# Feed-forward weights loaded in three pieces under cross attention, new orders for its last two steps, and other banks for the first feed-forward tile

## The reference

```
x = layernorm(x + self_attention(x))
x = layernorm(x + cross_attention(x, context) + bo)   # softmax(q k^T / 8) v, then Wo
g = silu(bitlinear(x, w_gate)); u = bitlinear(x, w_up)
x = layernorm(x + bitlinear(g * u, w_down))           # F = 2048
# bitlinear: the rows of x rounded to 8 bits by their own maximum, the weights to -1, 0, 1
```

## Time and profile before

| | us |
|---|---|
| median of 3 runs | 1890.73 (1886.93 to 1893.66) |
| the profiled execution, its own time | 1889.15 |
| its span, first to last instruction | 1887.4 |
| PE busy in the span | 1784.9 (95%) |
| DVE busy | 1445.7 (77%) |
| ACT busy | 1181.5 (63%) |
| POOL busy | 1039.0 (55%) |

### The profile page before, as it was taken

One profiled execution on the slowest core, in us unless ns is written; L12 is line 12 of the kernel. 1 busy time (PEld: TensorE's weight loads), 2 busy tenths in 40 slices (PEclk: granted clock), 3 DMA queues, 4 the chain that ended last, 5 costly groups with the idle time before them and its releaser, 6 DMA issues.

```text
span 1887.4 us, 43032 instructions
## 1 busy us (share of the span) xinstructions
PE 1784.9 (95%) x14128; PEld 1495.1 (79%) x14154; DVE 1445.7 (77%) x3366; ACT 1181.5 (63%) x2696; POOL 1039.0 (55%) x1169
## 2 busy tenths in 40 slices
PE   6899998999999899999999999999999999979997
PEld 4677776777777689999999998899999999964443
DVE  5667667788888777877777788878777877778887
ACT  4676776657656566666666666666566656655664
POOL 0343342334433348767866854587787877542554
PEclk9899998999999899999999999999999999989999
DMA  3322233101103233234324433223313331271221
GB/s 119 119 85 72 65 114 107 39 31 39 49 29 110 86 122 128 75 121 144 98 69 144 130 121 91 79 73 91 110 55 108 91 110 48 66 162 44 64 67 61
DMA packets 109574, 166.80 MB, mean 88 GB/s; under 512 B 32488, under 2 KB 67672, under 8 KB 109512
## 3 DMA queue, kind: packets, MB, share of 16 engines
q1 hardware_dynamic: 91016, 129.77, 22.1%
q0 software_dynamic: 14656, 28.92, 5.5%
q10 hardware_dynamic: 3840, 7.34, 1.2%
HBM read 109.25 MB, written 50.46 MB: 85 GB/s over the span
## 4 chain that ended last, share of the span: by engine, by line
PE 58%; DVE 15%; issue 9%; DMA 7%; ACT 5%; POOL 4%; SPq 1%; POOLq 0%; DVEq 0%; ACTq 0%
PE att_ps_P L1539 5%; PE att_ps_SA L1563 5%; PE att_ps_P L1527 4%; PE att_ps_P L1588 4%; PE att_ps_T L451 3%; PE att_ps_T L1527 3%; PE att_ps_O L1527 3%; PE att_ps_T L1539 3%; PE att_ps_P L1577 3%; DVE sa_sums L751 3%; PE att_ps_O L1539 2%; PE att_ps_P L1599 2%; PE att_ps_SB L513 2%; PE att_ps_T L1588 2%; DMA out_dram<-ff_y_out 2%
## 5 line engine op out<-in xcount | busy, mean ns | idle before, releaser
L1365 POOL TENSOR_TENSOR ca_pr<-ca_pr,ca_rec 112x750 f32<-112x750 f32 x256 | 367.0, 1454 | 212.7 <-DVE ca_rec L1814 209.6
L392 POOL TENSOR_TENSOR sa_p_lo<-sa_pr,sa_p_hi 112x448 fp32r<-112x448 f32 x128 | 147.8, 1160 | 331.7 <-ACT sa_p_hi L599 331.7
L1704 ACT ACTIVATE ca_big<-att_ps_P 126x384 fp32r<-126x384 f32 (+1 forms) x256 | 105.7, 448 | 68.3 <-PE att_ps_P L1577 66.8
L751 DVE RECIPROCAL sa_sums<-sa_sums 128x224 f32<-128x224 f32 x64 | 99.2, 1550 | 47.0 <-ACT sa_sums L608 46.6
L1698 ACT ACTIVATE ca_pr<-att_ps_SA,ca_nmax 112x750 f32<-112x750 f32 x128 | 113.6, 888 | 20.0 <-DVE ca_nmax L1810 9.3
L1819 DVE TENSOR_TENSOR ca_big<-att_ps_P,ca_big 126x384 fp32r<-126x384 f32 (+1 forms) x256 | 120.4, 498 | 4.3 <-ACT ca_big L1704 4.1
L1810 DVE TENSOR_REDUCE ca_nmax<-att_ps_SA 112x1 f32<-112x752 f32 x128 | 119.1, 931 | 0.5 <-PE att_ps_SA L1563 0.4
L1810 DVE TENSOR_REDUCE ca_nmax<-att_ps_SB 112x1 f32<-112x752 f32 x128 | 119.1, 931 | 0.0
L1539 PE MATMUL att_ps_P<-ca_w_hi,ca_ct 128*126 128x256 f32 x576 | 118.1, 284 | 0.0
L1698 ACT ACTIVATE ca_pr<-att_ps_SB,ca_nmax 112x750 f32<-112x750 f32 x128 | 113.1, 884 | 0.0
L451 PE MATMUL att_ps_T<-sa_w_hi,sa_xt_hi 128*112 128x512 f32 x192 | 82.9, 432 | 17.1 <-DVE sa_qs L729 10.9
(11 more groups left out here) (342 smaller groups left out, 6656.6 us busy)
## 6 DMA issues: line engine op xcount, KB each, us to landing
ct_kept<-ca_ct SPq DMA_DIRECT2D x8, 1134.0 KB, 9.1
ca_ct<-ct_kept POOLq DMA_DIRECT2D x8, 1134.0 KB, 8.2
ct_kept<-ca_ct SPq DMA_DIRECT2D x8, 1116.0 KB, 11.8
ca_ct<-ct_kept POOLq DMA_DIRECT2D x8, 1116.0 KB, 10.3
sa_xin<-in_x_dram SPq DMA_DIRECT2D x16, 448.0 KB, 3.6
xt_kept<-ca_xt SPq DMA_DIRECT2D x8, 896.0 KB, 5.1
ca_xt<-xt_kept POOLq DMA_DIRECT2D x8, 896.0 KB, 5.0
ternary<-ca_stage SPq DMA_DIRECT2D x36, 172.0 KB, 1.9
```

Source lines behind the costliest of these rows:

```text
L392: pool.tensor_tensor(p_lo[:, h % NB, :], pr[:, h % NB, :], f32(p_hi[:, h % NB, :]), ALU.subtract).then_inc(p_split, 1)
L751: dve.reciprocal(sums[:, p % 2, :], sums[:, p % 2, :]).then_inc(inverted, 1)
L1365: pool.tensor_tensor(w, w, rec[:, h % PB, c:c + 1].to_broadcast([R, S]), ALU.mult).then_inc(norm_done, 1)
```

## The change

It has four parts.

1. The held weights are laid out so that each of the three feed-forward weights covers the hi and lo of one projection: gate lies on Wq's, up on Wk's and the rows' buffer, down on Wv's and the staging buffer. So each can be loaded when that one projection is through.
2. SP waits for Q3, K31 and V15 of the last batch apart and issues each transpose behind its own wait (`hold`). The first two now stand in the step of batch 6, ahead of that batch's store.
3. The step of batch 6 in group 1, which holds the projections of batch 7, has its own orders on all engines (the third list of each `ORDERS`). V13, V14 and V15 leave it for the tail, K31 comes forward, and the guess F4 (DVE) and the refining L (POOL) stand later. On PE this step is no longer the last turn of a loop but written out once more. The tail has new orders too: u0! to u3! stand ahead of Y0 and Y1, and the transposes of tile 1's rows (y!) are in it.
4. Tile 0's gate and up blocks go to three halves of SA and SB in turn, where before they took SB, T, P0 and P1. The small feed-forward buffers change places in SBUF.

```diff
-    w_hi = [in_held(f"w_hi{i}", [P, blocks_k[i], GC], F32R) for i in range(3)]
-    w_lo_at = [in_held.at + 4 * GC * sum(blocks_k[:i]) for i in range(3)]
-    w_lo = [in_held(f"w_lo{i}", [P, blocks_k[i], GC], F32R) for i in range(3)]
+    for i in range(3):
+        w_hi.append(in_held(f"w_hi{i}", [P, blocks_k[i], GC], F32R))
+        raw.append(nc.alloc_sbuf_tensor_at(f"ca_raw{i}", [P, blocks_k[i], GC], F32, offset=in_held.at))
+        w_lo.append(in_held(f"w_lo{i}", [P, blocks_k[i], GC], F32R))
+        if i == 1:
+            spare_at.append(in_held.at)
+            xin = in_held("xin", [R, 2, DM])
+        elif i == 2:
+            stage = in_held("stage", [P, 2, GC])
...
+    LAST = steps("""V13 T2.1 T3.1 S2.1 O2 O3 T4.0 S3.0 T5.0 V14 V15 T4.1 S3.1 T5.1 O4 T6.0 O5 x! ~ T7.0 u0! T6.1 T7.1 u1! O6
+                    O7 u2! y! u3! Y0 Y1""")
...
+        def hold(m, done, also=None):
+            w = ff_ternary[m]
+            sp.wait_ge(done.filled, done.nth_filled)
+            if also:
+                also()
+            sp.dma_start_transpose(ff_held[m][:, :].rearrange("p (k r) -> p k r", r=w.shape[0]), w).then_inc(held[m], 16)
...
+                    elif b == B - 2 and g + 1 == GROUPS:
+                        sp.wait_ge(ff_out, 16 * NW * WB * GROUPS)
+                        hold(0, step_of(b, g)("Q3"), ff_first)
+                        hold(1, step_of(b, g)("K31"))
                     elif b == B - 1:
...
+                        ff_second()
+                        hold(2, at_last_step(LATE[-1]))
...
+    first_ps = [psum["SB"][:, BANK:2 * BANK], psum["SA"][:, 0:BANK], psum["SB"][:, 0:BANK]]
...
+    def gate_up_bank(f, m, first):
+
+        return first_ps[(2 * f + m) % 3] if first else gu_ps[(2 * f + m) % 4]
```

More of the change, by code:

```diff
@@ L1047, in cross_attention @@
     assert sorted(FRONT_UNITS) == sorted(UNITS[0]) and sorted(UNITS[1]) == sorted(u for u in UNITS[0] if u[0:2] not in CACHED)
-    front_plan, plans, last_plan = banks(CROSS_FRONT, TURN[0:2], "T0.0"), [banks(order) for order in ORDERS], banks(LAST, own={"O5": "SB", "O7": "SB", "Y1": "SA"})
-    LOOPS = [B - 1, B]
+    LATE = kind_of(LAST, "V")
+    assert sorted(UNITS[2] + LATE) == sorted(UNITS[1]) and all(u[0:2] == "V1" for u in LATE)
+    front_plan, plans, last_plan = banks(CROSS_FRONT, TURN[0:2], "T0.0"), [banks(order) for order in ORDERS], banks(LAST)
+    LOOPS = [B - 1, B - 1, 1]
     def uses(plan, s):
@@ L1586, in values @@
             pe.wait_ge(split.drained, split.nth_drained)
+            if st is at_last_step and h == VH:
+                for u in LATE:
+                    pe.wait_ge(st(u).drained, st(u).nth_drained)
             for j in range(JC):
@@ L1638, in rest @@
                 with pe.Fori(0, looped(g)) as b:
-                    step(g, step_of(b, g), batch(b, g), batch(b, g, 1))
-                if g + 1 < GROUPS:
-                    step(g, step_of(B - 1, g), batch(B - 1, g), after(B - 1, g), (g + 1) * W)
+                    step(g, b, batch(b, g), batch(b, g, 1))
+                for b in range(looped(g), B if g + 1 < GROUPS else B - 1):
+                    step(g, b, batch(b, g), after(b, g), (g + 1) * W if b == B - 1 else 0)
             for name, _ in LAST:
@@ L1723, in scalar @@
                            T1.0b+ S2.0+ V10+ S3.0+ V11+ T0.1a+ T0.1b+ T1.1a+ T1.1b+ S2.1+ S3.1+ V12+ O0+ O1+ T2.0a+ T2.0b+
-                           T3.0a+ T3.0b+ S4.0+ V13+ S5.0+ K31+ V14+ V15+""")]
+                           T3.0a+ T3.0b+ S4.0+ V13+ S5.0+ K31+ V14+ V15+"""),
+                  steps("""T2.1a T2.1b T3.1a T3.1b S4.1 Q0+ S5.1 Q1+ O2 O3 Q2+ T4.0a T4.0b T5.0a T5.0b S6.0 S7.0 K00+ V00+ K01+
+                          T4.1a T4.1b T5.1a T5.1b S6.1 Q3+ S7.1 V01+ O4 V02+ O5 V03+ K10+ T6.0a T6.0b T7.0a T7.0b S0.0+ S1.0+
+                          K11+ K20+ K21+ V04+ T6.1a T6.1b T7.1a T7.1b S0.1+ S1.1+ K30+ O6 O7 T0.0a+ T0.0b+ T1.0a+ T1.0b+ S2.0+
+                          S3.0+ K31+ V05+ V10+ T0.1a+ T0.1b+ T1.1a+ T1.1b+ S2.1+ S3.1+ V11+ O0+ O1+ T2.0a+ T2.0b+ T3.0a+
+                          T3.0b+ S4.0+ V12+ S5.0+""")]
         def do(name, at, st):
@@ L2166, in first @@
                 transpose_x(0)
+            elif name == "y":
+                transpose_x(1)
             else:
@@ L2173, in tile @@
         def tile(t, first=False, ahead=True):
-            gate_up(t, False, range(3))
+            if first:
+                pe.wait_ge(sg_done, FB)
+            for f in range(3):
+                if first:
+                    for ca_done in ca_free(f"v{f}"):
+                        pe.wait_ge(*ca_done)
+                gate_up(t, False, [f])
             if first:
```

120 lines of the change are left out of this document (60 added, 60 removed).

## The result

| | us |
|---|---|
| kernel before, median of 12 runs | 1888.96 (1886.56 to 1893.66) |
| changed kernel, median of 12 runs | 1893.12 (1890.55 to 1894.95) |
| ratio, 95% interval | 1.0023, 1.0015 to 1.0031 |
| profiled execution after, its own time and span | 1892.78 and 1891.0 |
| PE, DVE, ACT, POOL busy in it | 1786.5, 1448.1, 1182.4, 1040.8 |

The medians are 4.2 us apart. That is inside the bound of 0.3% which the prediction called no change, and inside its range, but the interval excludes one, and 1890.0 was too low. The profiled executions differ by 3.63 us.

The account below looks back on a forecast made before the run. PE was taken to bound the kernel up to 1664 us, then SP's transposes and DVE's order in the tail. From 1889.15, -0.7 at F5 and +1.7 for the clock gave 1890.2, forecast as 1890.0, range 1882.0 to 1896.0.

Parts of the forecast that it names:

- The long SP row: SP's issue of two transposes in the tail, 10.65 and 7.84 us, ahead of the load of tile 1's rows; forecast to leave the chain.
- the wait of next!: DVE's wait in the tail for the load of tile 1's rows; forecast to go wholly.
- The wait that takes the place of the old one: PE idle some 5.5 us after T2.1 at the end of batch 6's step, S2.1 starting 3.4 us later.
- both waits for L: DVE waits for POOL's L before F5 of batch 6, 2 to 3 us, and of batch 7, nearly 4.
- The slower rival: PE's clock falls a second time around T4.1, T5.1 and T6.0: +3.0 us, ending at 1893.8 to 1895.8; chance 0.21.
- the 1706 to 1709 that was called right: Start of tile 1 the new profile should show; 1706.2 at full clock, 6.1 us ahead of 1712.27.
- The clock behind the new hole: PE at half speed for 6 us over T3.1, S2.1, O2 and O3; 1.7 us taken, felt at S3.0.
- F5 (1.57) ends at 1669.5: F5 of batch 6 on DVE, taken at 1.57 us behind L, ending at 1669.5 where before 1666.2.
- The leg of 17.8 us: From the end of batch 7's F5 through SP's queue to tile 3 on PE, carried over unchanged at 17.8 us.
- The wait of 6.04 us: PE's idle time before O6 in the tail, laid to the late transposes; forecast to go wholly.
- Forecast +1.0: Net change at the end: -0.7 us at the last F5 and +1.7 for the clock.

Follow-up runs that it names:

- the run with Y ahead: Changed kernel with the tail's Y0 and Y1 ahead of u2! on PE and DVE, and the last F5 behind h!: 1889.20 us, ratio 1.0009.
- the guess early: Changed kernel with batch 6's guess F4 right behind F3 on DVE and L ahead of B0+ on POOL: 1889.64 us, ratio 1.0005.
- The kernel that is 7.4 us faster: Changed kernel with guess and L early, residual and tile 3's rows ahead of batch 7's store, v2! and v3! ahead of last F5: 1881.69 us, ratio 0.9961.
- The two kernels with both edits: Changed kernel with batch 6's guess and L early and the tail's Y0 and Y1 ahead of u2!: 1884.53 us; with the rows ahead besides, 1884.86 us.
- the rows ahead: Tile 0's residual and tile 3's rows loaded ahead of batch 7's store: on the kernel before 1886.91 us, on the changed kernel 1889.62 us.
- the run with L ahead of B: Changed kernel with only L moved ahead of B0+ on POOL in batch 6's step, the guess left late: 1890.31 us, ratio 1.0015.
- The queue alone: Kernel before with only the new weight layout and SP's new queue, all other engines' orders and banks unchanged: 1891.20 us, ratio 1.0025.
- one transpose early: Kernel before with the new weight layout and only gate's transpose moved into batch 6's step, up's behind tile 0's rows: 1883.76 us, ratio 0.9982.

## Why the prediction was wrong, by its steps

**Right.** The long SP row and the wait of next! are gone (it starts at 1691.25 with no idle time). K31 ended at 1646.5 (forecast near 1647), and the second transpose was issued by 1654.1. The step of batch 6 lost next to nothing: its last maxima end at 1663.90, forecast near 1663.97. The wait that takes the place of the old one is where it was put, and both waits for L bind.

**The slower rival came true by a part.** The clock did fall a second time among T4.1, T5.1 and T6.0, at 1687 to 1690, and made O4 2.58 us long; at full clock it took 1.47 (the run with Y ahead). But the clock was back before u0, so this cost some 1.1 us and not the 3.0 of the rival. With F5's 1.8 and 1.5 for the first spell (both below) it puts tile 1 at 1710.6. Tile 1 started at 1710.49, outside the 1706 to 1709 that was called right.

**The clock behind the new hole.** The forecast was 1.7 us at S3.0. Without it S3.0 would have been at 1675.2; it starts at 1678.45, and 1.8 of these 3.25 us are F5's, so 1.5 are the clock's. The size was right. The cause was not: with the guess early the hole is 1.94 us, and there is still a spell at 0.50, in which PE works 3.4 us. The kernel that is 7.4 us faster has it too:

```profile
1665.00:1667.00 2.00, 2.00 (x22) 2.00 (x24) 1.30 (x4) 0.79 (x2) 2.00 (x2) 0.50 0.73 226
```

Nor does the order of the instructions fix it. The two kernels with both edits, without and with the rows ahead, differ in nothing ahead of 1689 us, and PE stands 1.94 us ahead of T3.1 in both. The windows behind that hole, the first of the kernel without, the second of the one with the rows:

```profile
1666.00:1672.00 6.00, 5.89 (x32) 5.17 (x33) 3.78 (x9) 2.20 (x6) 3.16 (x3) 0.50 0.50 153
1666.00:1672.00 6.00, 4.83 (x48) 3.99 (x48) 5.03 (x10) 2.92 (x7) 4.08 (x4) 1.00 0.44 142
```

S3.0 follows S2.1 by 6.65 us in the first and by 5.01 in the second. So such a spell costs 1.6 us here, which is the size of the forecast, and whether it comes is not settled by the hole: three of the four executions with a hole of 1.9 us have it. All five with a hole of 4.5 us or more have it. The forecast of 1.7 was luck as far as it named the long hole as what must bring it; what decides it stays open.

**The first F5: the first term that was mis-sized.** The step "F5 (1.57) ends at 1669.5" took its price from the row of before. The change moved L, and with it what POOL does next: N4.0 and N5.0 begin 0.09 us after F5. It took 3.39 us. That is 1.8 us over the row of before. At the last F5 it is still 1.7: this F5 was forecast to end at 1719.0 to 1719.4 and 1.7 more for the clock, and ends at 1722.62. The run with L ahead of B shows the same term by itself: 1.7.

**The leg of 17.8 us: the step that failed.** "Then the same 17.8 us to tile 3" read a distance as a chain. In the kernel before, tile 3 stood at the end of PE's own work: 25.4 us from tile 1 with 1.9 us of short waits in it, 0.5 of them behind DVE's wait for the rows, and the run with the rows ahead gained 0.7 us there and nothing in the time. DVE's 2.21 us wait for the rows was hidden. In the changed kernel PE came to tile 2 3.2 us earlier and F5 ended 2.7 later, so two chains from F5 took over. One is DVE's own: tile 1's third and fourth product stand behind F5, ACT's scaling and silu behind them, and PE waits 3.59 us for that. It still does so with the rows ahead. The other is SP's: DVE's wait for tile 3's rows holds its next product, and PE waits 2.45 us for that; with the rows ahead this wait is gone. From the start of tile 2 to that of tile 3 it is 20.35 us where it was 12.15. Of these 8.2 more 5.5 are the holes and some 2.4 the clock, since PE did 4.76 us of work at 0.50. So the leg became 20.1. The prediction warned of low clock in the tail and not behind it.

**The sum again.** Forecast +1.0; 1.8 for the first F5 and 2.3 for the leg make +5.1, and tile 3 did start 5.0 us later. From tile 3 to the end were 149.7 us before and 148.3 after, which leaves 3.6. This last stretch is 148.2 to 149.4 in all my other kernels, so I count its 1.4 us to the execution and not to the change. The traces bear that out: before has PE at 0.50 with 5.8 us of work near the end (from 1871.8), the changed kernel has no such spell there, and the other kernel with as long a one is the one with 149.4. That the measured profiles stand only 3.6 apart is thus luck by 1.4 us; the medians are 4.2 apart.

**The gain that was credited.** That the wait of 6.04 us "goes wholly" held, but the reason given, the transposes, was the smaller part. The queue alone is a loss with K31 late, and a gain of 3.4 us with one transpose early. The rest must be DVE's new order, in which the rounding of tile 0 stands before T4.1; this is read from the orders, and no run has that order alone.
